# A two-way selective scan with a routed gate: one state's products change engine, and the segment edge moves into the step sizes

## The reference

```
s = scan(xn; forward weights) + reverse(scan(reverse(xn); backward weights))
g = silu(xn + 0.3 * (expert_ffn(xn) @ Wo + bo))
out = x + s * g
```

## Time and profile before

| | |
|---|---|
| median of 3 runs | 3227.8 us (3227.16 to 3228.38) |
| the profiled execution | 3226.65 us |
| its span, first to last instruction | 3224.9 us |
| mean granted clock of TensorE | 0.927 |
| first scan | at 78.86 us |
| last scan | at 3211.30 us |

### The profile page before, as it was taken

The page is one execution under the profiler, slowest core; times in us unless marked ns, Lnnn a source line. Parts: engine busy times, 40 slices in busy tenths (PEclk is TensorE's granted clock), DMA queues, the critical chain, the costliest instruction groups (busy, mean ns, idle before and its releaser), DMA issues. The chain is left out here.

```text
span 3224.9 us, 49367 instructions
## 1 busy us (share of the span) xinstructions
PE 2521.8 (78%) x15766; PEld 2012.3 (62%) x15766; DVE 3075.3 (95%) x2027; ACT 2924.0 (91%) x5498; POOL 3009.2 (93%) x1422
## 2 busy tenths in 40 slices
PE   7778778877777787788777788877787787787776
PEld 5666656666666666566666566665666665666665
DVE  3899999999999999999999999999999999999999
ACT  4899999999999999999999999999999999999985
POOL 2899999999999999999999999999999999999997
PEclk9999999899899989999998999899999989998998
DMA  5443344433344433344433444433444333444331
GB/s 161 143 123 118 107 129 127 137 121 118 104 130 135 128 119 119 109 133 133 127 114 109 130 127 136 120 120 104 129 134 132 115 118 110 133 133 126 111 118 53
DMA packets 273367, 394.19 MB, mean 122 GB/s; under 512 B 45003, under 2 KB 119508, under 8 KB 273108
## 3 DMA queue, kind: packets, MB, share of 16 engines
q1 hardware_dynamic: 273108, 391.03, 40.0%
HBM read 348.98 MB, written 25.18 MB: 116 GB/s over the span
## 5 line engine op out<-in xcount | busy, mean ns | idle before, releaser
L476 POOL TENSOR_TENSOR bx<-dx,b_sb 128x1024 f32<-128x1024 f32 x608 | 1439.5, 2384 | 21.9 <-DVE hs L868 21.0
L868 DVE TENSOR_TENSOR_SCAN hs<-decay,bx 128x1024 f32<-128x1024 f32 x608 | 1384.1, 2281 | 45.1 <-issue 35.8
L1100 PE MATMUL y<-ident,hc 128*128 128x128 f32 x8192 | 1111.0, 286 | 37.5 <-DVE hc L843 37.1
L1100 PEld LDWEIGHTS y<-ident,hc 128*128 128x128 f32 x8192 | 991.4, 148 | 146.2 <-DVE hc L843 95.5
L464 POOL TENSOR_TENSOR hc<-hs,c_sb 128x1024 f32<-128x1024 f32 x448 | 1057.4, 2371 | 15.9 <-DVE hs L868 15.6
L868 DVE TENSOR_TENSOR_SCAN hs<-decay_sb,decay 128x1024 f32<-128x1024 f32 x416 | 936.5, 2270 | 16.3 <-ACT decay_sb L731 12.4
L731 ACT ACTIVATE decay<-delta,rate 128x511 f32<-128x511 f32 (+1 forms) x1216 | 785.5, 683 | 55.3 <-DVE hs L868 53.9
L587 ACT ACTIVATE dxb<-dxT,btok 128x256 f32<-128x256 f32 x1664 | 706.5, 500 | 0.0
L843 DVE TENSOR_TENSOR hc<-hs,c 128x1024 f32<-128x1024 f32 x576 | 689.6, 1197 | 3.0 <-PE c L1083 1.6
L1075 PE MATMUL decay<-ident,dxb 128*128 128x128 f32 x3328 | 450.8, 280 | 244.6 <-DVE hs L868 223.4
L1075 PEld LDWEIGHTS decay<-ident,dxb 128*128 128x128 f32 x3328 | 375.3, 143 | 374.8 <-issue 306.9
(11 more groups left out here) (126 smaller groups left out, 2192.5 us busy)
## 6 DMA issues: line engine op xcount, KB each, us to landing
b_sb<-b_scratch SPq DMA_DIRECT2D x608, 256.0 KB, 3.2
c_sb<-b_scratch SPq DMA_DIRECT2D x448, 256.0 KB, 3.5
xin<-in_L_attn_x_dram SPq DMA_DIRECT2D x32, 512.0 KB, 6.0
w_sb<-in_L_ffn_W_dram SPq DMA_DIRECT2D x32, 512.0 KB, 3.5
w2o_sb<-w2o_scratch SPq DMA_DIRECT2D x32, 512.0 KB
xres<-in_L_attn_x_dram SPq DMA_DIRECT2D x32, 512.0 KB, 5.3
out_dram<-og SPq DMA_DIRECT2D x32, 512.0 KB, 4.3
dbc<-high SPq DMA_DIRECT2D x64, 128.0 KB, 2.3
```

Source lines behind the costliest of these rows:

```text
L476: nc.gpsimd.tensor_tensor(bx[:, i % RING, :, :], dx[:, g, :, :], b_sb[:, i % BRING, :].unsqueeze(1).broadcast_to([P, DT, T]), ALU.mult).th ...
L868: V.tensor_tensor_scan(hs[:, s % HSLOTS, :, :].rearrange("p k t -> p (k t)")[:, u], factor.rearrange("p k t -> p (k t)")[:, u], data.rearr ...
L1100: ins = M(yps[:, c, k * P:(k + 1) * P], hc[:, s % RING, k, c * P:(c + 1) * P], ident[:, :], start=False, stop=(s == ADDED[-1]), is_transpo ...
```

## The change

State 29 goes from `POOL_B` to `TURNED`: its input is scaled on ScalarE (at step 24) and turned by TensorE. State 24 goes to `POOL_C`: its product with C is made on GpSimd. The edge column is no longer written into decays: after dx is made, GpSimd writes 1e20 into that column of delta (`cut`, a one-column memset, steps 29 and 44), so that the exponential of rate times it is zero in each decay; rates are kept at or below -1e-16 for this. Every decay then has all 512 columns, the edge semaphores go, and the first decay of a group waits for the cut. Decays 29 and 30 are made at ScalarE's steps 26 and 27, the next row's decay 5 at step 29. At steps 30 and 31 ScalarE makes the decay before it copies dx, where before this held for step 30 alone. The residual sum moves from GpSimd's step 3 to step 4.

```diff
--- before.py
+++ after.py
@@ -39,25 +39,24 @@
     B_TURN, B_COPY = 11, 13
     EXPAND, ABS = (14, 15, 24, 25), (16, 17, 26, 27)
     EXP, LN, SQUARE, RATIO = (18, 27), (19, 28), (20, 29), (21, 30)
-    LOG1P, STEPSIZE, DX = (25, 36), (27, 39), (28, 43)
+    LOG1P, STEPSIZE, DX, CUT = (25, 36), (27, 39), (28, 43), (29, 44)
     DX_TURN, DX_COPY = (28, 29, 44, 45), (30, 31, 46, 47)
     FFN_IN, HIDDEN, GELU = (16, 16, 18, 18, 20, 20, 22, 22), (18, 20, 22, 24), 31
     FFN_OUT, GATE = (31, 31, 32, 32, 34, 34, 35, 35), (35, 38)
     FFN_OUT_FIRST, GATE_FIRST = (33, 33, 34, 34, 36, 36, 37, 37), (36, 38)
-    Y_OUT, Y_RESIDUAL = 1, 3
+    Y_OUT, Y_RESIDUAL = 1, 4
     SKIP = {0: ((0, 0), (2, 0)), 1: ((0, 1), (1, 0), (1, 1), (2, 1)), 4: ((3, 0), (3, 1))}
 
-    TURNED, SCALED_AT, TURN_LEAD = (5, 6, 8, 9, 11, 13, 14, 15, 22, 24, 26, 28, 30), (1, 2, 3, 4, 5, 7, 9, 10, 17, 19, 21, 23, 25), 3
+    TURNED, SCALED_AT, TURN_LEAD = (5, 6, 8, 9, 11, 13, 14, 15, 22, 24, 26, 28, 29, 30), (1, 2, 3, 4, 5, 7, 9, 10, 17, 19, 21, 23, 24, 25), 3
     POOL_B = [s for s in range(STEPS) if s not in TURNED]
-    POOL_C, C_LAG, ADD_LAG = (2, 4, 5, 7, 9, 10, 11, 12, 16, 18, 20, 22, 26, 27), 4, 2
+    POOL_C, C_LAG, ADD_LAG = (2, 4, 5, 7, 9, 10, 11, 12, 16, 18, 20, 22, 24, 26, 27), 4, 2
     ON_DVE = [s for s in range(STEPS) if s not in POOL_C]
     NT, NBX, ND, NPC = len(TURNED), len(POOL_B), len(ON_DVE), len(POOL_C)
     ADDED = [s for i in range(STEPS + ADD_LAG) for s in ((i - ADD_LAG,) if i - ADD_LAG in POOL_C else ()) + ((i,) if i in ON_DVE else ())]
     FIRST_TURNED = [next(i for i, s in enumerate(TURNED) if s >= g * N) for g in range(2)]
-    EDGED_SB = [s for s in TURNED if TURNED.index(s) - FIRST_TURNED[s // N] < TSLOTS]
-    EDGED = [s for s in POOL_B if s % N < DSLOTS or s - DSLOTS in TURNED]
-
-    AHEAD = {14: 22, 15: 24, 16: 26, 23: 28}
+    NO_CARRY, LEAST_RATE = 1e20, 1e-16
+
+    AHEAD, AHEAD_NEXT = {14: 22, 15: 24, 16: 26, 23: 28, 26: 29, 27: 30}, {29: 5}
     EPS = 1e-5
 
 
@@ -204,8 +203,7 @@
         s_proj, s_bstored = sem("projected_copied"), sem("b_stored")
         s_bsb, s_bx = [sem(f"b_loaded{i}") for i in range(BRING)], sem("bx_done")
         s_decay, s_scan, s_cps, s_hc, s_red = (sem(n) for n in ("decay_done", "scan_done", "c_psum", "hc_done", "sum_states_done"))
-        s_edge, s_diag = sem("segment_edges"), sem("skip_diagonal")
-        s_edge_sb, s_decay_sb = sem("segment_edges_turned"), sem("decay_turned_done")
+        s_cut, s_diag, s_decay_sb = sem("delta_cut"), sem("skip_diagonal"), sem("decay_turned_done")
         s_csb, s_hcp = [sem(f"c_loaded{i}") for i in range(CRING)], sem("hc_pool_done")
         s_bturn, s_btok = sem("b_turned"), sem("b_tokens_copied")
         s_dxturn, s_dxT = sem("dx_turned"), sem("dx_tokens_copied")
@@ -446,6 +444,12 @@
                 wait(pool, s_dxturn, (row - 1) * 2 * DT + g * DT + DT)
                 nc.gpsimd.tensor_tensor(dx[:, g, :, :], delta[:, g * (1 + par), :, :], xnT[:, par, :, :], ALU.mult).then_inc(s_dx, 1)
 
+            def cut(row, par, g):
+
+                pool.wait_ge(s_dx, row * 2 + g + 1)
+                later, edge = (1, 0) if g == 0 else (0, T - 1)
+                nc.gpsimd.memset(delta[:, g * (1 + par), later, edge:edge + 1], NO_CARRY).then_inc(s_cut, 1)
+
             def log1p(row, g):
                 pool.wait_ge(s_ratio, row * 2 + g + 1)
                 nc.gpsimd.tensor_tensor(lg[:, :, :], lg[:, :, :], ex[:, g, :, :], ALU.mult).then_inc(s_log1p, 1)
@@ -504,11 +508,14 @@
                     step_size(row, par, STEPSIZE.index(s))
                 if s in DX:
                     step_x(row, par, DX.index(s))
+                if s in CUT:
+                    cut(row, par, CUT.index(s))
 
             shift_of(0)
             log1p(0, 0)
             step_size(0, 0, 0)
             step_x(0, 0, 0)
+            cut(0, 0, 0)
 
             def body(row, par, last):
                 for s in range(STEPS):
@@ -726,33 +733,21 @@
             copy_dxT(0, 1)
             def decay_of(row, par, s, to, k):
                 g, n = s // N, s % N
-                later = 1 - g
-                cols = slice(0, T) if k != later else slice(1, T) if g == 0 else slice(0, T - 1)
-                return A(to[:, k, cols], delta[:, g * (1 + par), k, cols], ACT.Exp, scale=rate[:, g, k, n:n + 1])
-
-            def cut_of(s, to):
-                later, edge = (1, 0) if s < N else (0, T - 1)
-                return A(to[:, later, edge:edge + 1], eps[:, :], ACT.Identity, scale=0.0)
+                return A(to[:, k, :], delta[:, g * (1 + par), k, :], ACT.Exp, scale=rate[:, g, k, n:n + 1])
 
             def make_decay(row, par, s):
 
-                act.wait_ge(s_delta, row * 2 + s // N + 1)
+                act.wait_ge(s_cut, row * 2 + s // N + 1)
                 if s in TURNED:
                     i = row * NT + TURNED.index(s)
                     used = i - TSLOTS
                     wait(act, s_scan, used // NT * STEPS + TURNED[used % NT] + 1)
-                    to = decay_sb[:, i % TSLOTS, :, :]
-                    if s in EDGED_SB:
-                        cut_of(s, to).then_inc(s_edge_sb, 1)
                     for k in range(DT):
-                        decay_of(row, par, s, to, k).then_inc(s_decay_sb, 1)
+                        decay_of(row, par, s, decay_sb[:, i % TSLOTS, :, :], k).then_inc(s_decay_sb, 1)
                 else:
                     wait(act, s_scan, row * STEPS + s - DSLOTS + 1)
-                    to = dps[s % DSLOTS]
-                    if s in EDGED:
-                        cut_of(s, to).then_inc(s_edge, 1)
                     for k in range(DT):
-                        decay_of(row, par, s, to, k).then_inc(s_decay, 1)
+                        decay_of(row, par, s, dps[s % DSLOTS], k).then_inc(s_decay, 1)
 
             act.wait_ge(s_rate, 1)
             act.wait_ge(s_w2oc, 2 * NE - 2)
@@ -768,15 +763,17 @@
                 for s in range(STEPS):
                     if s in AHEAD:
                         make_decay(row, par, AHEAD[s])
+                    if s in AHEAD_NEXT and not last:
+                        make_decay(row + 1, 1 - par, AHEAD_NEXT[s])
                     drain(row, par, s + STEPS)
-                    if not last and s != DX_COPY[0]:
+                    if not last and s not in DX_COPY[:DT]:
                         drain(row + 1, 1 - par, s)
                     if s + DSLOTS < STEPS:
-                        if s + DSLOTS not in AHEAD.values():
+                        if s + DSLOTS not in AHEAD.values() and (row == 0 or s + DSLOTS not in AHEAD_NEXT.values()):
                             make_decay(row, par, s + DSLOTS)
                     elif not last:
                         make_decay(row + 1, 1 - par, s + DSLOTS - STEPS)
-                    if not last and s == DX_COPY[0]:
+                    if not last and s in DX_COPY[:DT]:
                         drain(row + 1, 1 - par, s)
                     if s in SCALED_AT:
                         scale_dx(row, par, SCALED_AT.index(s))
@@ -849,15 +846,11 @@
                 if s in TURNED:
                     i = row * NT + TURNED.index(s)
                     dve.wait_ge(s_bxT, i + 1)
-                    if s in EDGED_SB:
-                        dve.wait_ge(s_edge_sb, row * len(EDGED_SB) + EDGED_SB.index(s) + 1)
                     dve.wait_ge(s_decay_sb, DT * i + DT)
                     data, factor = dps[s % DSLOTS][:, :, :], decay_sb[:, i % TSLOTS, :, :]
                 else:
                     i = row * NBX + on_bx(s)
                     dve.wait_ge(s_bx, i + 1)
-                    if s in EDGED:
-                        dve.wait_ge(s_edge, row * len(EDGED) + EDGED.index(s) + 1)
                     dve.wait_ge(s_decay, DT * i + DT)
                     data, factor = bx[:, i % RING, :, :], dps[s % DSLOTS][:, :, :]
                 used = s - HSLOTS
@@ -904,7 +897,7 @@
             low_part(0)
             dve.wait_ge(s_aexp, 1)
             V.tensor_scalar(rate[:, :, :, :].rearrange("p a k n -> p (a k n)"), rate[:, :, :, :].rearrange("p a k n -> p (a k n)"),
-                            -1.0, None, ALU.mult).then_inc(s_rate, 1)
+                            -1.0, -LEAST_RATE, ALU.mult, ALU.min).then_inc(s_rate, 1)
             V.tensor_tensor(dsum[:, :], dskip[:, 0, :], dskip[:, 1, :], ALU.add).then_inc(s_dsum, 1)
             dve.wait_ge(s_dsum, 1)
             for k in range(DT):
```

## The result

The changed kernel takes 3155.1 us (median of 4 runs, 3152.8 to 3156.9) against 3227.9 before: ratio 0.9776, 95% interval 0.9763 to 0.9790. The forecast was 3159 us. Its profiled execution took 3155.45 us, its span 3153.7.

What follows compares the result with a forecast made beforehand. Loops through several engines, each 97.9 us a row, were taken as the bound; after the change VectorE alone came to 95.0, Loop G 95.5, Loop A 95.8, so -2.15 us a row, -68 us over 31.5 rows: 3159 us, range 3138 to 3194.

Steps and rivals of the forecast that it cites:

- Loop A: Product 15 on VectorE, ScalarE to the ratio, GpSimd's log1p to product 27, scan 31, next product 15: forecast 95.8 us, longest.
- three loops: VectorE alone, one through GpSimd, one through ScalarE as well; each checked to give 97.9 us a row before the change.
- Loop G: GpSimd's residual sum to product 27, then VectorE's scan 31 to the output product: 97.9 us before, forecast 95.5.
- Product 24 leaves VectorE: State 24's product with C moves to GpSimd: VectorE's own loop -1.11 us a row; GpSimd takes 2.38 us for such a product.
- Product 27 becomes late next: At scan 31: GpSimd ends product 27 about 0.8 us after VectorE is ready for that scan.
- The residual sum: On GpSimd, moved behind product 4 with B, which then runs in the 3.4 us wait: Loop G -2.33 us.
- Scan 13's wait goes, -0.5.: ScalarE has 1.22 us less before scan 13 with decay 5 made a row earlier, so VectorE's wait there goes: -0.5 us.
- Scan 1's wait: VectorE's wait at scan 1, counted with scan 2's as 1.2 us a row; scans 2 and 13 were forecast without waits.
- Decay 1 fills the wait ... 1.4 us earlier: ScalarE's decay 1 before the dx copy fills a 1.25 us wait; silu's table load 1.4 us earlier, scan 2's wait -0.95.
- The memsets: Two one-column memsets on GpSimd, taken at 0.1 us each, bounds 0.05 and 0.42; effect on ScalarE's decays: zero.
- rival 4: Slower: going from product to memset and back on GpSimd costs 1.5 us or more, 98.3 us a row, 3238 us; chance 0.04.
- Wrong if GpSimd idles over 1 us at log1p: Sign against the prediction: GpSimd idling over 1 us at log1p; a few tenths, waiting for the ratio, were expected.

Runs made afterwards that it cites:

- the old kernel with loop G opened: Kernel before with the residual sum at GpSimd's step 4 and, at ScalarE's step 31, decay 1 ahead of the copy of dx: 3190.6 us, ratio 0.9898.

## Why the prediction was right

By its steps:

- *The sum and the loop that sets it.* Right. Loop A was forecast at 95.8 and is 95.5, each part within 0.4 us, and moving the ratio moved the row. -2.15 us a row was forecast, -2.43 measured by medians and -2.27 by means. That three loops each gave 97.9 before proved less than it seems: the waits were in the sums, and with them any way round comes to the row. Loop G's 0.36 us from product 27 to scan 31 was not all hand-over: where scan 31 does wait, it is 0.13.
- *Product 24 leaves VectorE; "Product 27 becomes late next".* Right: 0.65 to 0.75 us of waiting at scan 31 for 0.8 forecast. With product 24 back on VectorE the row is only 0.3 us longer in the mean, so this half of the swap is worth little; with state 29's product back on GpSimd it is 2.5 us longer in the mean, so the other half has to be there. The Trainium skill (GPSIMD Engine Reference, Engine selection) would keep product 24 on VectorE; the durations agree with it (2.36 to 1.20 us), the row does not, by 0.3 us, and the intervals of the two ratios just touch.
- *The residual sum.* Right that loop G would decide without it, wrong in the size: "-2.33" counted product 4 alone. GpSimd's step 4 also makes the log1p product ahead of the residual sum, so two products moved, and "about 1 us" of waiting became none. Loop G was not the bound either way.
- *"Scan 13's wait goes, -0.5."* This step failed. The wait is still 0.50 us. ScalarE does get ahead of decay 7, but there it now waits 1.3 us for scan 5, and from decay 7 to decay 13 it works without a pause for 19 us as before. What it gains earlier than its last wait is lost in it. That decay 5 in its own place costs nothing says the same, and moving state 15's scalings from between that wait and decay 13 to behind it removed the wait at scan 13.
- *Scan 1's wait.* Not in the sum at all: "scan 1" was left at its 0.26. It went, with 0.08 of overlap: +0.34 us, which made up for most of scan 13. It belongs to the edge copies, as the kernel with the edge alone shows. With it, scan 2's wait, the gate's and the one at low, the stretch from scan 31 to product 15 shrank by 2.26 us, for 1.85 forecast.
- *"Decay 1 fills the wait ... 1.4 us earlier".* The effect was right (the table load came from 2.7 to 0.9 us after scan 0 in the mean, scan 2's wait went), and on the old kernel with loop G opened the order does it. In the changed kernel the cause is mostly another: the order is worth 0.3 us of the table load and nothing of the row, for TensorE's transposes of dx come earlier against scan 0. They follow product 28's end by 6.8 us in every row, where before it was 6.7, 7.4 and 8.0 in turn (7.35 in the mean), and scan 0 comes 0.7 us later behind product 28 because scan 31 waits. Scan 2's wait before went with those three times: 0.3, 1.0 and 1.4 us. The row used for the prediction is one with 8.0, so its "1.25 us" ahead of the copy was more than the mean of 0.93.
- *The memsets.* Right, 0.10 us each, and rival 4 is out. The 6 us that the Trainium skill (GPSIMD Engine Reference, Instruction dispatch) names for a first call are not paid at a memset within the rows. The transposes of 29 are hidden as said: scan 29 waits for nothing.
- *"Wrong if GpSimd idles over 1 us at log1p".* It idles 1.01 in the mean, so taken strictly this sign came though the mechanism held. GpSimd came earlier than forecast, by the second product moved; ScalarE's 21.38 us are as forecast. It is where loop A waits for its part on ScalarE: with the ratio 1.6 us earlier most of it went, and the row was 0.7 us shorter.

The first scan, at 78.9 us before and 81.5 after, is at 77.9 to 83.4 in the other profiles, in no order that follows an edit, so nothing is put down to the change there.

What stays open: why TensorE's transposes of dx end at three different times behind product 28 in the rows before, and at one after.

## What to carry to other kernels

When several engines are over 90% busy, look for the loops: follow one period from an engine's instruction through each hand-over back to the same instruction, and add up. The sum alone proves nothing, for with its waits it always comes to the period; a loop is closed where each hand-over is as short as in a kernel that waits there in every row. A change wins what it takes out of the longest loop, down to the second longest, so edits must be judged together: here one that won nothing alone won 1.3 us a row with a second, and each of three edits of the change can be left out by itself without loss (all three together were not left out). And a gain ahead of an engine's last wait in the loop is lost in that wait: what stands between that wait and the late instruction is what has to be moved.

## What the runs showed of the hardware

**An extra wait instruction came with 0.34 us.** With the edge wait of scan 1 there is 0.26 us of idle time ahead of it and no overlap, without it none, 0.34 us in all, right behind VectorE's wait for its own statistics. All three profiled kernels with the edge waits show the 0.26, and none of the eleven without. The edge copy itself was written over 3 us before. Elsewhere in the row the same extra waits cost nothing that shows. That it is the instruction which costs, and only behind a wait of that kind, is inferred: no run added a wait elsewhere.

**TensorE at the row's end.** The 16 additions of the row's last states took 3.62 us at a granted clock of 0.50 before. After, in two stretches (length, busy, granted clock, DMA share, GB/s) and as instructions:

```profile
1609.50:1613.30 3.80, 3.79 (x19) 0.58 0.20 64
1613.30:1616.40 3.10, 2.98 (x25) 0.97 0.03 12
```

```profile
1609.51 0.50 PE L1076 MATMUL c<-dbc,selector 128*128 128x512 f32 x1 [1.85 <-DVE hc L840]
1609.84 3.37 PE L1093 MATMUL y<-ident,hc 128*128 128x128 f32 x16
1613.01 0.85 PE L997 MATMUL front<-ident,dx 128*128 128x128 f32 x4
```

The idle time ahead of them is 1.85 us where it was 2.13 (in every third row 1.26), and the low level (1.2 of 2.4 GHz) was left sooner. Over the rows (300 to 3000 us) the 16 additions take 3.2 or 3.6 us before and 2.6 to 3.6 after. No run varied this alone, so it is not shown that the added transposes are the cause. But the kernel with decay 5 in its own place shows that it doesn't matter for the row. With the same 1.9 us of idle time ahead, the additions take 2.6 to 3.6 us in 13 of its first 17 rows and 1.91 us, at the full clock, in all later ones:

```profile
940.56 3.47 PE L1093 MATMUL y<-ident,hc 128*128 128x128 f32 x16
...
1894.87 1.91 PE L1093 MATMUL y<-ident,hc 128*128 128x128 f32 x16
```

```profile
940.50:944.10 3.60, 3.60 (x20) 0.55 0.17 60
1894.80:1896.80 2.00, 2.00 (x19) 1.00 0.00 0
```

The later rows last 95.5 to 95.6 us and the earlier ones mostly 95.4: the full clock there won nothing.
